# First cross attention of a Perceiver block: where the row statistics are turned, and how the last half ends

## The reference, cut to what matters

```
k, v = ctx @ Wk + bk, ctx @ Wv + bv            # 1585 keys of 256 channels
k = layernorm(k over the head's 32 channels)    # q as well, before
s = (q @ k.T) * 32 ** -0.5
p = softmax(s over the keys)
o = p @ v                                       # all heads, joined: 512 channels
x = x + (o + side_attention) @ Wo + bo
```

## Time and profile before

| | |
|---|---|
| median of 3 runs | 2482.18 us (2479.97 to 2484.78) |
| the profiled execution | 2479.76 us, span of its trace 2477.7 us |
| TensorE's mean granted clock in it | 0.953 of full |
| busy over the span | PE 90%, DVE 64%, ACT 48%, POOL 42% |

### The profile page before, as it was taken

How to read it: one execution, slowest core, us unless ns; L and a number is a source line. 1 busy time by engine, 2 the same in 40 slices (tenths; PEclk the granted TensorE clock), 3 DMA queues, 4 the chain that set the end, 5 groups by cost and what they waited for, 6 DMA issues and landing times. The chain is left out here.

```text
span 2477.7 us, 47145 instructions
## 1 busy us (share of the span) xinstructions
PE 2231.0 (90%) x16750; PEld 1759.6 (71%) x16756; DVE 1593.3 (64%) x2669; ACT 1186.3 (48%) x2264; POOL 1029.2 (42%) x707
## 2 busy tenths in 40 slices
PE   5699999999997799988998999999999998888866
PEld 2677777777774688866777688888888876666644
DVE  5367777777777333335423688888888884566663
ACT  2355656565653233322313666676666663233242
POOL 5168888888885000000100354455455451111320
PEclk8699999999996999989999999999999999899989
DMA  3000000001000221103303100000000001211200
GB/s 115 5 23 28 28 28 2 28 28 48 2 2 2 82 68 58 61 19 83 88 5 125 31 18 11 28 28 14 16 28 26 2 1 68 60 46 38 90 1 17
DMA packets 106424, 89.86 MB, mean 36 GB/s; under 512 B 33104, under 2 KB 86624, under 8 KB 106224
## 3 DMA queue, kind: packets, MB, share of 16 engines
q1 hardware_dynamic: 105936, 87.21, 11.6%
q0 software_dynamic: 288, 0.00, 0.0%
HBM read 86.15 MB, written 1.05 MB: 35 GB/s over the span
## 5 line engine op out<-in xcount | busy, mean ns | idle before, releaser
L2377 POOL TENSOR_TENSOR xT<-xT,x1b_ring 128x512 f32<-128x512 f32 (+1 forms) x176 | 248.2, 1410 | 212.6 <-ACT x1b_ring L2507 205.6
L1013 POOL TENSOR_TENSOR x0b_krstd<-x0b_krstd,minus_half 128x24 f32<-128x24 f32 x64 | 266.9, 4170 | 89.4 <-DVE x0b_krstd L1076 85.8
L1033 POOL TENSOR_TENSOR xT<-xT,x0b_ring 128x512 f32<-128x512 f32 (+1 forms) x170 | 239.7, 1410 | 40.2 <-ACT x0b_ring L1250 25.7
L111 DVE TENSOR_TENSOR x1b_plo<-x1b_ring,x1b_phi 128x512 fp32r<-128x512 f32 (+1 forms) x208 | 222.7, 1071 | 5.2 <-issue 4.9
L2522 ACT ACTIVATE x1b_ring<-x_ps,x1b_keymask 128x512 f32<-128x512 f32 (+1 forms) x208 | 142.9, 687 | 130.1 <-DVE xT L2449 125.0
L1250 ACT ACTIVATE x0b_ring<-x0b_ring 128x512 f32<-128x512 f32 (+1 forms) x208 | 131.2, 631 | 149.9 <-DVE x0b_ring L1094 141.7
L1126 DVE TENSOR_TENSOR x0b_ring<-x_ps,x0b_krstd 128x512 f32<-128x512 f32 (+1 forms) x208 | 142.9, 687 | 75.0 <-PE x_ps L918 73.9
L116 PE MATMUL x_ps<-x1b_qy,x1b_yT 128*128 128x512 f32 (+1 forms) x416 | 175.2, 421 | 4.3 <-ACT x1b_ring L2522 2.9
L2449 DVE SCALAR_TENSOR_TENSOR xT<-x_ps,x1b_keymask,xT 128x512 f32<-128x512 f32 (+1 forms) x176 | 131.2, 746 | 57.4 <-PE x_ps L118 56.4
L116 PE MATMUL x_ps<-x1b_phi,x1b_yv 128*128 128x512 f32 (+1 forms) x416 | 165.8, 399 | 1.5 <-ACT x1b_out_sb L2489 1.5
L118 PE MATMUL x_ps<-x1b_qy,x1b_yT 128*128 128x512 f32 (+1 forms) x416 | 163.8, 394 | 0.0
(11 more groups left out here) (596 smaller groups left out, 5660.2 us busy)
## 6 DMA issues: line engine op xcount, KB each, us to landing
x_y<-in_ctx_dram SPq DMA_DIRECT2D x8, 1536.0 KB
x_y<-in_ctx_dram SPq DMA_DIRECT2D x24, 512.0 KB, 3.8
a_wn<-in_L_attn_W_Q_dram SPq DMA_DIRECT2D x16, 256.0 KB, 3.0
a_wn<-in_L_attn_W_K_dram SPq DMA_DIRECT2D x16, 256.0 KB, 3.5
a_wn<-in_L_attn_W_V_dram SPq DMA_DIRECT2D x16, 256.0 KB, 4.0
a_won<-in_L_attn_W_O_dram SPq DMA_DIRECT2D x16, 256.0 KB, 2.9
x1a_wq<-in_L_xattn_Wq_dram SPq DMA_DIRECT2D x8, 512.0 KB, 8.9
x1c_wo<-in_L_xattn_Wo_dram SPq DMA_DIRECT2D x8, 512.0 KB, 7.1
```

What stands on the lines that cost most here:

```text
L111: return v.tensor_tensor(lo, exact, hi.bitcast(F32), ALU.subtract)
L1013: ins = g_.tensor_tensor(r, r, c.minus_half[:, 0:8].unsqueeze(1).broadcast_to([P, whole, 8]), ALU.pow)
L1033: g_.tensor_tensor(total[half][0:m, :], old, src, ALU.add).then_inc(summed, 1)
L2377: g_.tensor_tensor(total[half][0:m, :], old, src, ALU.add).then_inc(summed, 1)
```

## The change: what it does

1. In every step PE and DVE work through their lists in another order. Before, PE did "sums" and "inverse" ahead of a step's scores and "maxima" right behind them. Now "maxima" stands behind what `HERE` makes and ahead of what `AHEAD` makes, and "sums" and "inverse" stand behind both, ahead of the value product. DVE takes its results in the same new order, and the banks are handed out in it.
2. In the last half of the last sequence the row sums of tiles from `LATE` = 17 on are no longer added by DVE. PE multiplies each of these tiles, and the sum of the earlier ones (`total[1]`), by a matrix of ones (L1042 in the new file) into one PSUM bank, in the layout of the output; DVE inverts that 128x128 piece (L1246) and multiplies. The transposes of the last "sums" and "inverse" and two steps are gone.
3. The stage x0c is gone. Of the projection, three of the four token tiles are done by PE in the drain steps (`PROJECT`: 4 products at step 26, 2 at step 27, one each at steps 28 to 33), the fourth at the very end. The bias is added by POOL, behind its last row sums; DVE adds two products before the last inverse, two behind it.

```diff
-            for n in range(TILES + 19 if part == "last" else TILES):
-
-                for what, at in (("sums", 30), ("inverse", 31), ("maxima", 13)):
+            for n in range(LAST if part == "last" else TILES):
+
+                for ahead, e in made_at(part, n):
+                    if not ahead:
+                        put((seq, e))
+                f = half_at(part, n, 13)
+                if f is not None:
+                    put(("maxima", 2 * seq + f))
+                for ahead, e in made_at(part, n):
+                    if ahead:
+                        put((seq + 1, e))
+                for what, at in (("sums", 30), ("inverse", 31)):
                     f = half_at(part, n, at)
                     if f is not None:
                         put((what, 2 * seq + f))
-                for ahead, e in made_at(part, n):
-                    put((seq + ahead, e))
+        put("late")
+        put("rest")
+        PROJECT = {TILES: 4, TILES + 1: 2, TILES + 2: 1, TILES + 3: 1, TILES + 4: 1, TILES + 5: 1, TILES + 6: 1, TILES + 7: 1}
+        pieces = iter([(t, g) for t in range(T - 1) for g in range(HG0)])
...
+                        if part == "last" and t >= LATE:
+                            bank, nth = place["late"]
+                            if t == LATE:
+                                pe.wait_ge(kv_free[bank], nth + 1)
+                            sources = [ring[0:m, slot_of(seq, t), :]]
+                            if t == TILES - 3:
+
+                                pe.wait_ge(summed, (KT - 1) * (2 * B - 1) + (LATE - KT - 1))
+                                sources.append(total[1])
+                            for src in sources:
+                                for h in range(8):
+                                    g, rows = h // 4, slice(32 * (h % 4), 32 * (h % 4) + 32)
+                                    mm = pe.matmul(ps[rows, bank, g * S:(g + 1) * S], ones[0:src.shape[0], :],
+                                                   src[:, h * S:(h + 1) * S], start=(t == LATE and g == 0),
+                                                   stop=(t == TILES - 1), skip_group_check=True)
...
+                def project(n):
+                    for _ in range(PROJECT.get(n, 0)):
+                        t, g = next(pieces)
+                        if (t, g) == (0, 0):
+                            pe.wait_ge(wo_loaded, 32)
+
+                            pe.wait_ge(added, 2 * B - 2)
+                        if g == 0:
+
+                            pe.wait_ge(kept, TILES * B - len(S_BANKS) + 1 + t)
+                        mm = pe.matmul(ps[:, out_bank(t), :], ctxT[:, g, t * P:(t + 1) * P], wo[:, g, :],
+                                       start=(g == 0), stop=(g == HG0 - 1))
...
+                g_.wait_ge(wo_loaded, 32)
+                for t in range(T):
+                    g_.tensor_tensor(c.X[:, t, :], c.X[:, t, :], bo[:, :], ALU.add).then_inc(biased, 1)
...
-                    t = lagged(part, n, LAG_SUB + 1)
-                    if part == "last" and t is not None and t >= LATE:
...
-                        v.tensor_tensor(total[1][0:m, :], total[1][0:m, :], ring[0:m, slot_of(seq, t), :], ALU.add
-                                        ).then_inc(summed, 1)
...
+                add_output(0)
+                add_output(1)
+                heads = lambda bank: ps[:, bank, 0:2 * S].rearrange("p (g n) -> p g n", g=2)
+                v.wait_ge(late_done, 1)
+                v.reciprocal(late_inverse[:, :, :], heads(place["late"][0])).then_inc(late_inverted, 1)
+                v.wait_ge(late_inverted, 1)
+                v.wait_ge(pv_done, TILES * B)
+                v.wait_ge(added, 2 * B - 1)
+                v.tensor_tensor(osb[:, :, :], heads(O_BANK), late_inverse[:, :, :], ALU.mult).then_inc(late_normed, 1)
+                v.wait_ge(late_normed, 1)
+                o = ctxT[:, 2:4, (B - 1) * S:B * S]
+                v.tensor_tensor(o, osb[:, :, :], o, ALU.add).then_inc(added, 1)
+                add_output(2)
+                add_output(T - 1)
```

More of the change, by code:

```diff
@@ L825, in slot_of, with out_bank @@
             return (TILES * seq + t) % SLOTS
+        def out_bank(t):
+            return S_BANKS[(TILES * B - len(S_BANKS) + t) % len(S_BANKS)] if t < T - 1 else place["rest"][0]
         def steps(before, step):
@@ L936, in step @@
                         mm.then_inc(max_spread, 1)
+                    if n < TILES:
+                        after = part != "last" or n < TILES - 1
+                        if after:
+                            begin_scores(*((seq, n + 1) if n < TILES - 1 else (seq + 1, 0)))
+                        pe.wait_ge(begun, TILES * seq + n + 1)
+                        for g in range(2):
+                            mm = scores(seq, n, g, 1)
+                            if g == 1:
+                                mm.then_inc(scored, 1)
+                            if after:
+                                mm = scores(*((seq, n + 1) if n < TILES - 1 else (seq + 1, 0)), g, 0)
+                        if after:
+                            mm.then_inc(begun, 1)
+                    for ahead, e in made_at(part, n):
+                        if not ahead:
+                            make(seq, e)
+                    if n == TILES:
+                        project(n)
+                    f = half_at(part, n, 13)
+                    if f is not None:
+                        bank, nth = place["maxima", 2 * seq + f]
+                        pe.wait_ge(kv_free[bank], nth + 1)
+                        pe.wait_ge(max_done, (KT - 1) * (2 * seq + f + 1))
+                        for t in range(4):
+                            mm = pe.transpose(ps[:, bank, t * P:(t + 1) * P], run[f % 2][:, t * P:(t + 1) * P], c.ident[:, :])
+                        mm.then_inc(max_flipped, 1)
+                        pe.sem_inc(kv_full[bank], 1)
+                    for ahead, e in made_at(part, n):
+                        if ahead:
+                            make(seq + 1, e)
                     f = half_at(part, n, 30)
@@ L1005, in _ @@
+                steps(lambda e: make(0, e), step)
+                bank, nth = place["rest"]
+                pe.wait_ge(kv_free[bank], nth + 1)
+                pe.wait_ge(added, 2 * B)
+                for g in range(HG0):
+                    mm = pe.matmul(ps[:, bank, :], ctxT[:, g, (T - 1) * P:T * P], wo[:, g, :],
+                                   start=(g == 0), stop=(g == HG0 - 1))
+                mm.then_inc(projected, 1)
             @block.gpsimd
@@ L1136, in step @@
                             v.tensor_tensor(run[half][0:m, :], before, slot, ALU.max).then_inc(max_done, 1)
+                    for ahead, e in made_at(part, n):
+                        if not ahead:
+                            take(seq, e)
                     f = half_at(part, n, 13)
@@ L1149, in step @@
                         v.tensor_tensor(top, top, q, ALU.subtract).then_inc(rowmax_done, 1)
+                    for ahead, e in made_at(part, n):
+                        if ahead:
+                            take(seq + 1, e)
+                    f = half_at(part, n, 30)
+                    if f is not None:
+                        inv = inverse[:, f % 2, :]
+                        v.wait_ge(sum_flipped, 2 * seq + f + 3)
+                        bank = place["sums", 2 * seq + f][0]
+                        v.tensor_reduce(inv, four(ps[:, bank, :]), AX.X, ALU.add).then_inc(rowsum_done, 1)
+                        v.wait_ge(rowsum_done, 2 * (2 * seq + f) + 1)
+                        v.sem_inc(kv_free[bank], 1)
+                        v.reciprocal(inv, inv).then_inc(rowsum_done, 1)
                     f = half_at(part, n, 31)
```

87 lines of the change are left out of this document (22 added, 65 removed).

## The result

| | before | changed |
|---|---|---|
| median of the runs | 2482.69 us (2479.97 to 2484.78, 4 runs) | 2452.99 us (2450.61 to 2456.55, 4 runs) |
| ratio, 95% interval | 1 | 0.9883 (0.9872 to 0.9895) |
| profiled execution | 2479.76 us, span 2477.7 | 2456.55 us, span 2454.6 |

The change makes the kernel 29.7 us faster (26 to 32 by the interval); 2453.5 us had been forecast. The size came out right, and so did most of its parts. That the two figures agree to 0.5 us is luck all the same: the stage itself gained 3.8 us more than my sum, and the single executions scatter by as much behind it.

What follows compares the result with a forecast made beforehand. PE was taken to set the sequences' pace, with 3.3 us of waits each, and DVE the end's. 3.5 + 6.6 - 1.4 + 20.0 = 28.7 us gave 2453.5 us; own range 2446 to 2462, with two rivals 2442 to 2466.

Steps and rivals of the forecast that it cites:

- Step 0: Maxima, 7 sequences: PE waits for ACT's copy instead of DVE's last maximum; 0.5 us gained each, 3.5 us.
- Steps 17 to 19: Sums and inverse, 6 sequences: waits filled, but DVE can follow by only 1.1 us each; 6.6 us gained.
- Step 14: The price: the next key product waits for a bank until ACT has squared; 0.2 us, 7 times, 1.4 us lost.
- my 8.7: Sum of the terms for the steps in the sequences: 3.5 + 6.6 - 1.4 = 8.7 us gained.
- The tail: End of the last sequence and projection: the end comes 20.0 us sooner, bounds 15 to 22.4.
- my 5.1 us: Tail: time of the four remaining projection products, the middle between 3.4 us at full clock and 6.8 at half.
- POOL beside the subtractions: Tail: by the shared-port rule nine subtractions beside POOL could take 10 us more; by the rows nothing is added.
- The waits only move: Rival: time is lost at another bank in the sequences, only the tail counts; 2462 us, chance 0.15.
- The waits go altogether: Rival: all PE waits in the sequences vanish, 7 x 3.3 = 23 us and the tail; 2439 to 2445 us, chance 0.16.
- Given back in part: Rival: projection products hold up the drain, or POOL's bias is late; 2467 to 2484 us, chance 0.04.
- Slower by the clock: Rival: joined waits of about 2.2 us drop PE to half clock, twice a sequence 40 us lost; 2502 us, chance 0.03.
- my 28.7: Whole gain forecast, sequences and tail: 3.5 + 6.6 - 1.4 + 20.0 = 28.7 us.

Runs made afterwards that it cites:

- the maxima alone: Kernel before with only the maxima moved behind the products for the same sequence, old tail: 2477.9 us, ratio 0.9978.
- second profile: The kernel before, unaltered, profiled again: x0 ends 0.7 us earlier than in its first profile, the program 3.0 us later.
- the repeated changed kernel: The changed kernel run again, unaltered: 2450.8 us, ratio 0.9879 to the kernel before.
- the one with three edits: Changed kernel, two swaps (K030 ahead of T02, K010 ahead of T00) and two last projection products ahead of the last half's wait: 2445.2 us, ratio 0.9854.
- the kernel with the old order: Changed kernel with the new tail but the steps' order of the kernel before: 2466.7 us, ratio 0.9933.
- the sums alone: Kernel before with only sums and inverses moved behind the step's products, old tail: 2477.1 us, ratio 0.9972.

## Why the prediction came out

**Step 0: the wait right, its worth smaller.** PE starts on T02 at 441.21 behind a wait of 1.08 us for ACT's copy. 1.57 - 1.08 is the 0.5 us of the sum, and the maxima behind it don't wait. By the starts of the scores, step 1 gains 0.3 us of it.

**Steps 17 to 19: right in the sum, and more fragile than I wrote.** The key product waits 0.30 us for the bank (0.36 forecast) and T00 0.33 for ACT's copy. By the starts of the scores 1.3 us are won between steps 16 and 26, for the 1.1 of the sum. A sequence is 80.90 us long, and 80.9 was forecast. But the terms are not independent, as the text had them: 0.95 for the sums and 0.2 for the maxima alone, 1.5 together.

**Step 14: right in kind, about half in size.** The key product there starts at 484.00, directly behind the scores, but its weights do wait 0.18 us for ACT, which ends its square at 483.91:

```profile
484.00 0.19 PEld L116 LDWEIGHTS x_ps<-x0b_yT,x_wkv 128*128 128x128 f32 x1 [0.18 <-ACTq L1277]
```

By the starts of the scores the step costs about 0.1 us and not 0.2. The wait of PE itself for ACT's square, 0.2 us in the list of the changed kernel (L900), is another one, at 474.39, and the kernel before has it too:

```profile
PE x_ps L876 <- ACT x0b_sq L1188: 0.2, 1, 0.2
```

**The clock that comes back: a term that was missing.** "The last sequence has no next one to make keys for, and there DVE sets the pace, so 6 x 1.1" was wrong: the wait for the inverse falls from 2.22 to 1.30 us, the clock doesn't fall, and 3.7 us are won between step 13 and the last maxima against the first profile of before, 2.2 against the second. I had read the half clock of 748.65 as a price of the tail and asked only whether new waits would cause it, not whether an old one would stop. The sum for the sequences has the same gap: I read one sequence in the middle, and the second one, with its 1.92 us and half clock, holds 0.8 of the 2.2 us by which 10.9 exceeds my 8.7. The seventh distance holds 0.6, the sixth 0.4, which is one long sequence of before (82.94 us, and 82.38 in its second profile), and the other four 0.1 each.

**The tail: right, with two errors that cancel, which is luck.** Counted from the last maxima's transposes it is 19.6 us shorter; my 20.0 held 0.7 us from the steps ahead of them. Moved to the old count (12.9 us later), the subtractions start at 780.9 (780.1 forecast) and take 5.46 us for nine (5.4), the reciprocal starts at 789.4 (about 787.4) and takes 0.96 (0.95), the last four products take 3.67 (5.1), the end is at 795.6 (795.2). Of the 2.0 us by which the reciprocal is late, 0.8 are there already at the subtractions. The other 1.2 arise on PE, which stood still for 1.22 us ahead of the last tiles' products, waiting for nothing that the profile shows (0.96 in the repeated changed kernel, 1.54 in the one with three edits). The 1.4 us won back are the clock: it stayed full behind a wait of 1.82 us in both profiles of the changed kernel; behind the same wait in the kernel with the old order it was half for a part and the products took 5.37. So my 5.1 us, the middle between full clock and half clock, came near the one case and missed the other; half clock for all eight, 6.8 us, happened in neither.

**POOL beside the subtractions: as the rows said.** Nine subtractions follow one another at 0.60 us beside POOL's four additions of 1.27 us, and nothing slows them; the rows of the kernel before that do stretch, to 1.85 us, are DVE's running maxima, with both operands in SBUF. The Trainium skill (GPSIMD Engine Reference, section 2, Architecture) states that the ports are shared with VectorE; that this slows every VectorE instruction was my reading of it. The same page of the Trainium skill, in its section 1, Specifications, names only VectorE instructions in a 2-port mode or with two SBUF inputs as contending. The trace agrees with that: the subtractions, with one operand in PSUM, take 0.69 us at most.

**The rivals.** "The waits only move" is false of this change and true of the next one, the two swaps in the steps. "The waits go altogether" failed at ACT's copy and the bank, as its counter-argument said: 2.1 us of 3.5 are left, the 0.2 for the square counted. "Given back in part" doesn't show in the tail. "Slower by the clock" didn't happen in the changed kernel; the sums alone have it in three sequences of seven, behind waits of 1.9 us, where I had thought of one of 2.2. The stage's 32.5 us exceed my 28.7 by 3.8: 3.7 in the last sequence, where the term was missing, 2.2 in the sequences before it, less 1.2 by which the stage began late and 0.9 in the tail. The medians' 29.7 lie lower than that; the single profiles scatter by some 3 us behind the stage, and 1.5 of the 3.7 is scatter of before. So the forecast hit the median with a term missing, and scatter hid it.

## What to carry to other kernels

A wait before a statistic's transposes can be filled with products from the same step, but price the moves together: one of two can leave a longer wait at the other place (1.9 us for 1.6 here), and that may cost the clock. When a profile shows half clock behind a wait, ask of every edit that shortens the wait whether the clock comes back, and book that as a term of its own. In a tail, put products whose inputs are complete ahead of the wait for the last one; where the loop is steady, check a filled wait by the distance of two iterations and not by the wait's own row.

## What I had not expected

- The clock's answer to idle PE isn't the same each time. Behind 1.30 and 1.57 us it never fell. Waits of 1.89 to 1.92 us stand at step 0 in the profiles with the old place of the maxima: it fell behind all four in the second sequence and behind two of the five later ones with the sums alone moved. Behind 1.82 us it stayed full in two executions and was lower in a third. Behind 2.22 us it fell in all four profiles that have this wait: in one of before it fell 0.9 us ahead of the wait's end, in the other 0.7 us behind it.
- A 128x128 reciprocal costs 0.96 us, 3.3 times an addition of that size (0.29). From 128x4 with its 0.178 us it is 6.3 ns for each further element of a partition, the slope between 4 and 16 elements.
- 16 value products and 16 products with ones together take 0.45 us, start to start, while they alternate in the tail; they come faster than the subtractions' 0.60 us, and PE is late there only for the gap of 1.2 us.
- Two executions of the same kernel differ by 3.7 us (before) and 5.8 us (changed) in the unchanged stages behind x0b.
